# A fused attention and mixture-of-experts layer on one core: six pairs' values with buffers of their own, and the sixth pair ahead of the first scores

## The reference

```python
x = x + layernorm(attention(layernorm(x)))      # x: 8 x 1024 x 256, 16 heads of 16, causal
x = x + layernorm(moe(layernorm(x)))            # 8 experts of 512, the best 2 of each token

q, k, v = (einsum('oi,bsi->bso', W, x) for W in (Wq, Wk, Wv))
score = where(causal, q @ k.T / sqrt(16), -inf)
out = softmax(score) @ v @ Wo.T
```

## Time and profile before

| | before |
|---|---|
| median of 3 runs | 2091.95 us (2091.38 to 2093.63) |
| profiled execution | 2092.46 us, span 2090.8 us |
| TensorE busy | 1953.0 us, 93% |
| VectorE busy | 1585.5 us, 76% |
| ScalarE busy | 1335.6 us, 64% |
| GpSimd busy | 946.2 us, 45% |
| granted TensorE clock, mean | 0.977 of full |

### The profile page before, as it was taken

One profiled execution on the slowest core, in us unless ns is written; L12 is line 12 of the kernel. 1 busy time (PEld: TensorE's weight loads), 2 busy tenths in 40 slices (PEclk: granted clock), 3 DMA queues, 4 the chain that ended last, 5 costly groups with the idle time before them and its releaser, 6 DMA issues. The chain is left out here.

```text
span 2090.8 us, 50256 instructions
## 1 busy us (share of the span) xinstructions
PE 1953.0 (93%) x13588; PEld 1297.9 (62%) x13589; DVE 1585.5 (76%) x5416; ACT 1335.6 (64%) x3405; POOL 946.2 (45%) x1440
## 2 busy tenths in 40 slices
PE   6799999999999999999999889999999999999970
PEld 4344444444444444444433338999999999999970
DVE  2877788888888888888788837778777777777757
ACT  3377777777777777777777685555444555544436
POOL 5233344455655646556455553454333333333327
PEclk9899999999999999999999999999999999999995
DMA  6633546465454554545445458888989999998868
GB/s 200 197 112 122 179 145 209 141 188 175 148 180 133 174 158 146 181 129 169 148 137 189 138 181 239 246 238 249 265 258 256 268 258 262 261 266 241 238 191 322
DMA packets 259188, 414.81 MB, mean 198 GB/s; under 512 B 37040, under 2 KB 194992, under 8 KB 251824
## 3 DMA queue, kind: packets, MB, share of 16 engines
q1 hardware_dynamic: 219520, 368.19, 54.7%
q0 software_dynamic: 29680, 35.41, 9.6%
q10 hardware_dynamic: 9792, 8.93, 1.4%
HBM read 289.55 MB, written 122.28 MB: 197 GB/s over the span
## 5 line engine op out<-in xcount | busy, mean ns | idle before, releaser
L1014 ACT ACTIVATE arena<-ps_e 128x512 f32<-128x512 f32 (+3 forms) x1536 | 687.2, 493 | 275.0 <-PE ps_e L1234 264.7
L649 DVE CUSTOM_DVE_ANT_0 arena<-ps_s,c 128x128 bf16<-128x128 f32 (+3 forms) x1024 | 479.1, 480 | 61.2 <-PE ps_s L1215 57.3
L1215 PE MATMUL ps_s<-arena 96*128 96x512 bf16 (+3 forms) x1536 | 487.6, 332 | 26.6 <-DMA arena<-qk_parts 6.9
L1234 PE MATMUL ps_e<-arena 98*128 98x512 bf16 (+3 forms) x1536 | 482.6, 328 | 3.5 <-ACT arena L1014 3.1
L652 DVE TENSOR_REDUCE cmax<-ps_s 128x1 f32<-128x512 f32 x512 | 351.2, 686 | 141.2 <-PE ps_s L1215 137.7
L1215 PEld LDWEIGHTS ps_s<-arena 96*128 96x128 bf16 x1536 | 151.7, 100 | 356.7 <-DVE cmax L649 91.8
L1253 PE MATMUL ps_o<-arena 128*32 128x512 f32 (+3 forms) x3072 | 328.8, 500 | 5.9 <-ACT ot L1028 3.5
L546 POOL TENSOR_SCALAR_AFFINE_SELECT arena<-arena 128x512 f32<-128x512 f32 x256 | 163.3, 638 | 294.2 <-ACT arena L1014 293.9
L530 POOL DMA_INDIRECT acc<-blank,place_now x135 | 215.4, 1596 | 124.0 <-POOL place_now L525 77.0
L1369 PE MATMUL ps_s<-arena 128*128 128x128 f32 x2192 | 269.4, 276 | 0.0
L1369 PEld LDWEIGHTS ps_s<-arena 128*128 128x128 f32 x2192 | 263.4, 193 | 5.5 <-ACT arena L1156 0.6
(11 more groups left out here) (183 smaller groups left out, 3050.7 us busy)
## 6 DMA issues: line engine op xcount, KB each, us to landing
arena<-in_gate_up SPq DMA_DIRECT2D x93, 1024.0 KB, 6.0
arena<-qk_parts SPq DMA_DIRECT2D x384, 128.0 KB, 2.9
c_h<-in_gate_up SPq DMA_DIRECT2D x46, 1024.0 KB
qk_parts<-space SPq DMA_DIRECT2D x120, 192.0 KB, 3.3
d_xin<-xs SPq DMA_DIRECT2D x140, 130.5 KB, 3.1
v_aug<-space SPq DMA_DIRECT2D x32, 512.0 KB, 5.0
arena<-v_aug SPq DMA_DIRECT2D x32, 512.0 KB, 5.1
o_t<-ot SPq DMA_DIRECT2D x64, 256.0 KB, 2.7
```

The costliest lines, as they stand in the source:

```text
L649: dve.tensor_tensor_reduce(summed[:, m % RJ, 0:w], ps_s[:, m % RS, 0:w], after[:, HALF - w:HALF], 1.0, LOWEST, ALU.add, ALU.max, dst).then ...
L1014: act.activation(pw[:, n % RP, 0:w], ps_e[:, n % RE, 0:w], ACT.Exp, scale=SCALE).then_inc(e_done, 1)
L1215: pe.matmul(ps_s[:, m % RS, 0:w], qs[0:ROWS, slot, i * P:(i + 1) * P], ks[0:ROWS, slot, k0:k0 + w], start=True, stop=True).then_inc(s_scor ...
L1234: pe.matmul(ps_e[:, n % RE, 0:w], ks[0:ROWS_M, slot, j * P:(j + 1) * P], qs[0:ROWS_M, slot, q0:q0 + w], start=True, stop=True).then_inc(e_ ...
```

## The change

Five edits in the opening.

1. Pairs 0 to 5 are moved four slots ahead: turned over at -40, -37, -34, -31, -27, -20, values at -26 to -23, -21, -14. Pair 6 and all later ones stay. BEGIN stays at -18, so turning over pair 5 and the first half of its first product now stand ahead of the first scores.
2. Values of pairs 2 and 3 are put into arena columns 13312 to 15360 (inside `vs`), those of pairs 4 and 5 into pieces of `pw`. VectorE sets three more areas to one at the start. Value copies wait for the store of pair a - 2 only from pair 6 on; ScalarE waits in slot -1 until the values of pairs 4 and 5 are stored.
3. The ones of `ks` are written in three pieces, one for each of the three sets of heads, at slots -20, -12 and -9. TensorE waits in slot -1 for all three.
4. SyncE stores the queries and keys of pair 4 at slot -17 and of pair 5 at -13 (before -16 and -9), always after the block of slot BEGIN.
5. SyncE fetches x of pair 7 at slot -16, after the stores of pair 4 (before at slot -17, ahead of them).

```diff
-    A_AT = [BEGIN - 18 + 3 * a for a in range(EARLY)] + [BEGIN - 5, BEGIN + 2] + [NE * (a - 6) - 4 for a in range(6, PAIRS)]
-    V_AT = [BEGIN - 4 + a for a in range(EARLY)] + [start + 6 for start in A_AT[EARLY:]]
+    A_AT = [BEGIN - 22 + 3 * a for a in range(EARLY)] + [BEGIN - 9, BEGIN - 2] + [NE * (a - 6) - 4 for a in range(6, PAIRS)]
+    V_AT = [BEGIN - 8 + a for a in range(EARLY)] + [start + 6 for start in A_AT[EARLY:]]
...
+        def vout_of(a):
+            if 2 <= a < EARLY:
+                at = 13312 + (a - 2) * 1024
+            elif EARLY <= a < EARLY + 2:
+                at = 16384 + (6, 10)[a - EARLY] * HALF
+            else:
+                return vout[:, a % 2]
+            return arena[:, at:at + 1024].rearrange("p (s c h d) -> p s c h d", s=4, c=2, h=4)
...
-                             vout[:, u].rearrange("p s c h d -> p s (c h d)")).then_inc(v_out[u], 16)
+                             vout_of(a).rearrange("p s c h d -> p s (c h d)")).then_inc(v_out[u], 16)
...
-                for a in pairs_due(7, 9, g):
+                for a in due([max(start + (7 if a < FIRST_EVEN else 9), BEGIN + 1 if a >= EARLY else SLOTS.start) for a, start in enumerate(A_AT)], 0, g):
...
-                for a in pairs_due(-1, -9, g):
+                for a in due([BEGIN + 2 if a == 5 else start - (1 if a < FIRST_EVEN else 9) for a, start in enumerate(A_AT)], 0, g):
...
-                if g == BEGIN:
-                    pool.wait_ge(a_p3, 2 * EARLY + 1)
-                    pool.memset(ks[ROWS:ROWS_M], -1.0).then_inc(ones, 1)
-                    pool.wait_ge(ones, 1)
+                for u, (at, done_by, n) in enumerate(((BEGIN - 2, a_p3, 2 * EARLY + 2), (BEGIN + 6, a_p3, 2 * EARLY + 4), (BEGIN + 9, s_mlo, 2))):
+                    if g == at:
+                        pool.wait_ge(done_by, n)
+                        pool.memset(ks[ROWS:ROWS_M, u * 4:u * 4 + 4], -1.0).then_inc(ones, 1)
+                        pool.wait_ge(ones, u + 1)
...
-            dve.memset(vout, 1.0).then_inc(v_ones, 1)
+            dve.memset(vout, 1.0)
+            for a in range(EARLY, EARLY + 2):
+                dve.memset(vout_of(a), 1.0)
+            dve.memset(arena[:, 13312:15360], 1.0).then_inc(v_ones, 1)
...
+                if g == -1:
+                    for u in range(2):
+                        act.wait_ge(v_out[u], (EARLY + 2) // 2 * 16)
...
-                            if a >= 2:
+                            if a >= EARLY + 2:
                                 act.wait_ge(v_out[u], a // 2 * 16)
...
-                                last = act.activation(vout[:, u, :, t, :, 0:DH],
+                                last = act.activation(vout_of(a)[:, :, t, :, 0:DH],
...
-                    pe.wait_ge(ones, 1)
+                    pe.wait_ge(ones, SETS)
```

## The result

The changed kernel takes 2099.43 us (median, 2098.2 to 2103.05), the kernel before 2091.95 beside it: the ratio is 1.0036 with an interval of 1.0026 to 1.0047, so 5.4 to 9.8 us slower. The prediction had 2091.4 with an upper end of 2094.8. The profiled execution of the changed kernel took 2098.2 us, its span is 2096.5 against 2090.8, 5.7 us more.

A forecast was written before the change was run, and what follows sets the result against it. TensorE bounds most of the span, VectorE the opening from 56.60 to 82.13 us. Terms -0.8 (opening) and +0.3 (clock), others 0, sum to -0.5 us: 2091.4 us against the median 2091.95, range 2087.9 to 2094.8.

The forecast's parts named there:

- The buffers: Opening: value copies of pairs 2 to 5 stop waiting; first maximum at 53.9 us, VectorE 3.7 us sooner at slot -8.
- What is late next: Slot -8: x of pair 7 lands at 81.3 us, VectorE waits about 2.9, so 0.8 of 3.7 us remain.
- The least landing: Lower bound for x of pair 7: 77.6 us, with stores issued at 0.5 each and a 3.0 us fetch.
- The clock: TensorE in the opening: up to one head more at the low clock level, 0 to 0.8 us, taken as 0.3.
- The memsets: VectorE at the start: 3.5 us of added memsets, statistics still start at 7.70, cost 0 with 0.2 us to spare.
- Ones and ScalarE's wait in slot -1: Opening: at most 1.7 us of the second ones memset uncovered, cost 0; ScalarE's wait hidden by over 9 us.
- Carried to the end: After slot 0: program unchanged and TensorE bounds, so the opening's 0.5 us gain reaches the end.
- C: Rival: SyncE's next 24 loads take 0.89 us each, fetch lands at 86.8, loss 4.7 us (2096.7); chance 0.13.

The follow-up runs named there:

- e3: The changed kernel again, without edits, for a second trace: 2099.81 us, ratio 1.0039.
- e6: The changed kernel with GpSimd's first addition in the last stage waiting for VectorE's second shift: 2097.34 us, ratio 1.0022.
- e1: The changed kernel with x of pair 7 fetched behind the value stores, ahead of the second quad's heads: 2093.24 us, ratio 1.0006.
- e7: The changed kernel with both the early fetch of e1 and the last-stage wait of e6: 2093.53 us, ratio 1.0002.
- e2: The kernel before with only the fetch of x of pair 7 moved to slot -16, behind pair 4's stores: 2096.82 us, ratio 1.0026.
- e5: The kernel before with only the new value buffers, their memsets and ScalarE's waits: 2095.45 us, ratio 1.0016.
- e4: The kernel before again, without edits, for a second trace: 2091.78 us, ratio 0.9999.
- e8: The kernel before with GpSimd's first addition in the last stage waiting for VectorE's second shift: 2092.43 us, ratio 0.9998.

## Why the prediction was wrong, point by point

The forecast was 0.5 us faster, the measured median is 7.5 us slower. Its mechanism, VectorE's wait for x of pair 7, was right (2.9 us forecast, 4.35 measured). Three steps failed: the landing of that x (put at 81.3 us, measured 83.7, 85.0 and 84.2), the memsets' cost of nothing (measured 0.5 us at least), and the step that carries the opening's difference unchanged to the end (the last stage added 2.2 us).

*The buffers.* Right: the copy ran at 43.37 (43.27), the sixth pair's turned copy ended at 51.1 (52.1), first maximum at 53.80 (53.9), VectorE at slot -8 at 79.4 (78.4). So VectorE was there 2.8 us sooner than before in this trace, 1.4 in e3 and 4.0 in e6; without a new wait it was 2.4 to 4.2 sooner (e1 and the four traces of e7), around the 3.7 that I had.

*What is late next.* The mechanism and the place were right: VectorE's wait, with x as its releaser, in slot -8, shown from both sides by e1 and e2. The size was wrong, and this is the term that failed first. I had the landing at 81.3; it was 83.7 and, in the second trace, 85.0. The issue came at 77.0 (78.6), not 75.6, for SyncE won 1.1 us in its block, not 3.7: from the first load of heads to the loads of values it took 29.5 us in both traces of before and 28.4 in both of the changed kernel. The second group of head loads began at 55.0, not 53.5. The stores of pair 4 gave back 1.3 us in the first trace, with 3.3 in place of 4.6. I had priced four value stores at 2.2 us from two short ones, and 24 loads at an unchanged price; the first two did take 1.13 us, the other two took 2.50, and the next two loads 2.7. The landing then took 6.7 us, where my figure allowed 5.7. What e5 and e4 add: from its old place the fetch landed at 81.7 and 81.5, although it was issued 1.3 and 1.9 us sooner. Between its landing at 81.4 and its reader at 82.13 there was 0.7 us of slack; a gain over that had to move the fetch forward, and I moved it back. (The least landing, 77.6, does not come out of its own terms either: stores from 70.9, five issues of 0.5 and 3.0 us give 76.4. Nothing hangs on it.)

*The clock.* The sign was right and the size too small: from the statistics to the first score for the exponentials went 0.75 us more than before (0.5 in e3, 0.9 in e6) where I had 0.3. That the low stretch begins 14 us sooner is not the reason: e2, where it begins at 81 us with the slots of before, takes 16.96 us for this piece, the changed kernel 16.97, the kernel before 16.22. What goes with it is how long the clock stays low behind the statistics: 10.3 us before, 13.6 in the changed kernel and in e2, 15.4 in e5, which takes 17.46 us. The second trace of before has 13.1 and takes 16.73, so part of the 0.75 is chance. No run tests this by itself.

*The memsets.* This term failed as well. The three took 3.6 us where I had 3.5, but with 0.16 to 0.38 us between them, which the row of a single one could not show; VectorE's timeline of the changed kernel:

```profile
3.28 0.91 DVE L640 MEMSET arena<- 128x1024 f32 x1 [0.16 <-issue]
4.35 0.91 DVE L640 MEMSET arena<- 128x1024 f32 x1 [0.16 <-issue]
5.64 1.76 DVE L641 MEMSET arena<- 128x2048 f32 x1 [0.38 <-issue]
...
8.17 0.75 DVE L919 BATCH_NORM_STATS2 a_stats<-space 128x6 f32<-128x256 f32 x2
```

Statistics start at 8.17, 0.5 us late. In this pair of traces it seems to cost nothing: SyncE's loads of heads began at 43.69 against 43.65. But in that row of the kernel before x had landed late. The second trace of it shows:

```profile
5.92 0.75 DVE L906 BATCH_NORM_STATS2 a_stats<-space 128x6 f32<-128x256 f32 x2 [0.21 <-DMA space<-in_x]
```

In the four traces without the new memsets the statistics start at 5.92 (e4), 6.33 (e8), 6.79 (e2) and 7.70 us, and the loads of heads at 41.8, 42.7, 42.5 and 43.65; in the ten with them the statistics start at 8.17 or 8.18 in every one, and the loads at 43.1 to 44.6. By the means that is 1.5 us at the statistics and 1.1 us at the loads, which the buffers had to win back, so the term was not 0 but about 1 us. It is a comparison of traces; no run has the buffers with their memsets out of the way. The rule of the Trainium skill on memsets gave the right start (8.2) by a wrong price: a memset of 2048 columns again took 1.76 us.

*Ones and ScalarE's wait in slot -1.* As predicted: the second memset, at 68.39 for 3.51 us, held up the low part of the maxima by at most 1.4 us (until 71.98), the third, at 74.50, by at most 1.0 (until 78.09), both ahead of the wait of slot -8; ScalarE's first exponentials waited for TensorE alone.

*Carried to the end.* This step failed outright. I had said that after slot 0 nothing in the program changes, so that the opening's difference reaches the end. The last stage added 2.2 us that no edit touches (shown by e6), and about 1 us more came between the first exponentials and the last stage, no more than the spread of the traces. Sum of the trace: 2.3 + 1.2 + 2.2 = 5.7 us. The median says 7.5; the 1.8 us between come from which executions were traced: of the changed kernel the fastest, 1.2 us under its median, of the kernel before one 0.5 us over its median. The means of three traces each give 3.35 us in the opening and 1.1 behind it; with the 2.2 us of the last stage that is 6.6 of the 7.5 us. e2 shows the same gap, +2.0 in its trace and +5 by its median, and there too the fastest execution was traced.

*Rivals and range.* C was the right direction: SyncE is held up, though not by 24 slower loads but by the stores and the two loads behind them, 2.7 us. At the landing of 83.7 it gives +1.6 and with the clock +2.3, which the range held; the 3.35 us of the three traces would have been 0.5 over its end. The last stage was in no case of mine, and it takes the result well out of the range. I gave 0.10 to a loss of this size, but for another reason in part.

## What to carry to other kernels

When a wait is taken away from one engine, look at the transfers that this engine's next steps need, and where they stand in the issuing engine's order: a fetch moved behind 1.25 MB of stores cost more than the stall whose removal was the aim, and putting it in front gained 6 us back. A transfer that lands just ahead of its reader is a bound already, though no row calls it a wait. One trace is not a price: the start of 7.70 us that hid the memsets was the latest of four. And a shift of a few microseconds is not simply carried to the end, where two engines meet later on: look for places where a 0.16 us instruction can come to stand behind a 2.3 us one.

## What the runs showed of the hardware

An issue of SyncE is not of fixed price: an x fetch took 0.43 us at 74.64 and 2.46 us behind 2.75 MB issued in the 5 us before it; behind two or four value stores of 512 KB issued back to back, the next two issues, in some traces three (loads of 128 KB, and the x fetch in e1 and e7), took 1.1 to 1.4 us each in place of 0.59, in all ten traces with the new buffers.

VectorE's scalar_tensor_tensor on 4 columns took 0.16 us, or 2.31 us when GpSimd's addition of 1024 columns (2.33 us) had started 0.04 us before it (2.29 to 2.35 us in the five traces that have it). The Trainium skill has the rule, in SBUF — State Buffer, section Who interferes with whom: an instruction of VectorE with two SBUF inputs contends with an instruction of GpSimd that reads SBUF, and it is the order of issue that decides which one blocks. The trace agrees; what it adds is that ScalarE and GpSimd then stood 2.2 us each in a chain, so that all 2.2 us were lost.
